# Routed rows of a two-expert layer: weighted on their way out of PSUM and added to the output in device memory tile by tile, in place of a store, a gather and a mix at the end

## What is computed

```
xn     = layernorm(x2)                       # 1024 tokens, 512 numbers each
probs  = softmax(xn @ Wg)                    # 8 experts
topv, topi = top_k(probs, 2);  topv /= sum(topv)
shared = gelu(xn @ W1) @ W2                  # every token
moe    = sum over the token's two experts e of topv_e * (gelu(xn @ Wu[e]) @ Wd[e])
out    = x2 + shared + moe
```

## Time and profile before

| | |
|---|---|
| median of 3 runs | 1807.81 us (1804.14 to 1808.26) |
| profiled execution | 1820.21 us, of which the span of the core's instructions is 1818.4 us |
| mean granted clock of TensorE | 0.957 |
| TensorE matmuls | 1668.8 us busy, 92% of the span |
| TensorE weight loads | 1310.3 us, 72% |
| VectorE, ScalarE, GpSimd | 653.6, 649.2 and 518.5 us (36%, 36%, 29%) |
| device memory | 107.27 MB read, 27.00 MB written |

### The profile page before, as it was taken

How to read it: one execution, slowest core, us unless ns; L and a number is a source line. 1 busy time by engine, 2 the same in 40 slices (tenths; PEclk the granted TensorE clock), 3 DMA queues, 4 the chain that set the end, 5 groups by cost and what they waited for, 6 DMA issues and landing times. The chain is left out here.

```text
span 1818.4 us, 24358 instructions
## 1 busy us (share of the span) xinstructions
PE 1668.8 (92%) x9230; PEld 1310.3 (72%) x9231; DVE 653.6 (36%) x1065; ACT 649.2 (36%) x1184; POOL 518.5 (29%) x291
## 2 busy tenths in 40 slices
PE   3899999999999999999999999779776989999992
PEld 2587887887887887887887887534344768888882
DVE  4224424424424524524524524331443512122123
ACT  0134434434434434434434434314222314354520
POOL 4333033033033033033033030030111254484803
PEclk9999999999999999999999999889876989999996
DMA  7511011011011011111011100260001444465315
GB/s 260 184 47 47 30 46 46 29 46 46 29 46 46 29 46 46 29 46 46 29 46 46 29 23 0 77 241 1 1 1 58 165 147 127 133 202 162 133 40 156
DMA packets 69581, 134.66 MB, mean 74 GB/s; under 512 B 7152, under 2 KB 23600, under 8 KB 69552
## 3 DMA queue, kind: packets, MB, share of 16 engines
q1 hardware_dynamic: 36048, 92.07, 15.1%
q10 hardware_dynamic: 30944, 33.83, 5.8%
q0 software_dynamic: 2560, 8.39, 1.5%
HBM read 107.27 MB, written 27.00 MB: 74 GB/s over the span
## 5 line engine op out<-in xcount | busy, mean ns | idle before, releaser
L203 POOL TENSOR_TENSOR ctx_h<-stage,one 128x1024 fp32r<-128x1024 f32 x64 | 121.3, 1895 | 769.8 <-PE ps_t L254 753.6
L254 PE MATMUL ps_s<-ctx_h,wk 128*128 128x512 f32 x1024 | 321.3, 390 | 1.7 <-DVE kT L434 1.7
L254 PE MATMUL ps_t<-wv,ctx_h 128*128 128x512 f32 x1024 | 317.4, 391 | 3.7 <-ACT vt L391 3.7
L452 DVE TENSOR_TENSOR kT<-ps_s,kT 64x512 fp32r<-64x512 f32 x128 | 87.6, 684 | 449.4 <-ACT kT L386 448.6
L254 PEld LDWEIGHTS ps_t<-wv,ctx_h 128*128 128x128 f32 x1024 | 193.4, 189 | 44.5 <-ACT vt L391 4.1
L254 PEld LDWEIGHTS ps_s<-ctx_h,wk 128*128 128x128 f32 x1024 | 192.2, 188 | 42.1 <-issue 2.5
L460 DVE TENSOR_REDUCE smax<-ps_s 128x1 f32<-128x1024 f32 x128 | 150.6, 1219 | 145.9 <-PE ps_s L267 144.9
L254 PE MATMUL ps_t<-wv,ctx_l 128*128 128x512 f32 x512 | 200.1, 391 | 0.0
L254 PE MATMUL ps_s<-ctx_l,wk 128*128 128x512 f32 x512 | 199.2, 389 | 0.0
L377 ACT ACTIVATE probs<-ps_s,nmax 128x1024 f32<-128x1024 f32 x128 | 142.1, 1124 | 91.5 <-DVE nmax L463 91.5
L385 ACT ACTIVATE kT<-ps_s 64x512 fp32r<-64x512 f32 x128 | 76.0, 594 | 265.2 <-PE ps_s L254 248.8
(11 more groups left out here) (191 smaller groups left out, 2249.0 us busy)
## 6 DMA issues: line engine op xcount, KB each, us to landing
stage<-in_ctx_dram SPq DMA_DIRECT2D x64, 512.0 KB, 3.6
raw_u<-in_up_dram SPq DMA_DIRECT2D x36, 512.0 KB, 3.4
raw_d<-in_down_dram SPq DMA_DIRECT2D x36, 512.0 KB, 4.4
row<-rows_scratch ACTq DMA_DIRECT2D x31, 256.0 KB, 2.7
rows_scratch<-zero SPq DMA_DIRECT2D x25, 256.0 KB, 3.5
rows_scratch<-y ACTq DMA_DIRECT2D x22, 256.0 KB, 3.1
q_scratch<-kT ACTq DMA_DIRECT2D x4, 1024.0 KB, 5.9
qa<-q_scratch ACTq DMA_DIRECT2D x32, 128.0 KB, 2.9
```

Source lines behind the costliest of these rows:

```text
L203: nc.gpsimd.tensor_tensor(hi, stage[:, slot], one[:, 0:1].unsqueeze(2).broadcast_to([P, 2, QT]), ALU.mult).then_inc(hi_done, 1)
L254: mm = nc.tensor.matmul(out, w(c), m(c), start=(c + k == 0), stop=(c == DC - 1 and k == 2))
L452: nc.vector.tensor_tensor(kT[XD:P, 0, p, keys], ps_s[0:XD, p, :], kT[0:XD, 0, p, keys], ALU.subtract)
```

## The change

- A table `meta_dram` has for each slot of the routed tiles the token's number and its weight. SP fills it with the number 1024 (no token) and the weight 0; GpSimd then scatters the real entries with 16 indirect transfers, and SP loads the whole table into `tag`, 31 tiles by 128 rows of two numbers.
- VectorE evicts a routed tile from PSUM with a multiplication by the rows' weights, and copies the tile's 128 token numbers to `target`. It does so only when the add of the tile before has landed (`added`) and the table is in (`tags_in`).
- GpSimd adds `y` to the output in device memory with one indirect accumulating transfer per tile (`add_rows`); rows with number 1024 are out of bounds and left out. A one-column operation on `hold` stands ahead of it.
- SP stores `x2 + shared` as the output after each shared tile. The first six of these stores stand between the weight loads of sets 1 and 2, the last two behind set 2, then the load of `tag`, then sets 3 to 8.
- GpSimd makes the rests of an expert's up chunks, adds the first tile, makes the rests of the down chunks and adds the other tiles. It starts with set 2 only when the table is loaded and the eight output stores have landed.
- The store of `y`, the gathers, the mixing and the last eight stores are gone.

```diff
@@ SP @@
-            for s in range(1, E + 1):
+            def store_out(t):
+                sp.wait_ge(y_copied, t + (AHEAD + 1))
+                sp.dma_start(out_ap[t], x2[:, t, :]).then_inc(out_stored, 16)
+
+            sp.wait_ge(tags_set, 1)
+            sp.dma_start(meta_dram.rearrange("(p r) w -> p r w", p=P), pad[:, :, :]).then_inc(padded, 16)
+            load_raw(1)
+            for t in range(NT - 2):
+                store_out(t)
+            load_raw(2)
+            for t in range(NT - 2, NT):
+                store_out(t)
+            sp.wait_ge(added, 16 * 2 * NT)
+            sp.dma_start(tag[:, 0:MAX_TILES, :], meta_dram.rearrange("(r p) w -> p r w", p=P)).then_inc(tags_in, 16)
+            for s in range(3, E + 1):
                 load_raw(s)
-            for t in range(NT):
-                sp.wait_ge(mixed, 2 * (t + 1))
-                sp.dma_start(out_ap[t], x2[:, t, :]).then_inc(out_stored, 16)
             sp.wait_ge(out_stored, 16 * NT)
@@ GpSimd @@
+            def add_rows(t):
+                pool.wait_ge(y_copied, t + (AHEAD + 1))
+                nc.gpsimd.tensor_tensor(hold[:, bass.ds(t, 1)], hold[:, 0:1], hold[:, 0:1], ALU.add)
+                pool.indirect_dma_start(
+                    out=out_ap.rearrange("b t d -> (b t) d"),
+                    out_offset=bass.IndirectOffsetOnAxis(
+                        ap=target[:, :], axis=0),
+                    in_=y[:, :], in_offset=None, bounds_check=B * T - 1, oob_is_err=False,
+                    compute_op=ALU.add).then_inc(added, 16)
...
-            for s in range(1, E + 1):
-                weights_rest(s)
-            pool.wait_ge(lo_done, CH * (E + 1))
-            pool.wait_ge(rows_sent, 16 * 2 * NT)
-            end = pool.value_load(first_i[0:1, E:E + 1], min_val=NT, max_val=MAX_TILES)
-            pool.wait_ge(row_in, end * 16 + 32)
-            pool.wait_ge(y_stored, end * 16)
-
-            nc.gpsimd.tensor_tensor(hold[:, :], hold[:, :], hold[:, :], ALU.add)
+            weights_rest(1, range(CH))
+            pool.wait_ge(tags_set, 2)
+            pool.wait_ge(padded, 16)
             for t in range(NT):
                 for k in range(2):
                     pool.indirect_dma_start(
-                        out=picked[k][:, t, :], out_offset=None,
-                        in_=rows_dram.rearrange("n p d -> (n p) d"),
-                        in_offset=bass.IndirectOffsetOnAxis(ap=slot_i[:, k, t:t + 1], axis=0)).then_inc(got[t], 16)
+                        out=meta_dram, out_offset=bass.IndirectOffsetOnAxis(ap=slot_i[:, k, t:t + 1], axis=0),
+                        in_=tags[:, k, t, :], in_offset=None).then_inc(added, 16)
+            pool.wait_ge(firsts_done, 1)
+            pool.wait_ge(tags_in, 16)
+            pool.wait_ge(out_stored, 16 * NT)
+            for e in range(E):
+                lo, hi = bounds(pool, e)
+                if e + 2 <= E:
+                    weights_rest(e + 2, range(DC))
+                add_rows(lo)
+                if e + 2 <= E:
+                    weights_rest(e + 2, range(DC, CH))
+                with pool.Fori(lo + 1, hi) as t:
+                    add_rows(t)
+            end = pool.value_load(first_i[0:1, E:E + 1], min_val=NT, max_val=MAX_TILES)
+            pool.wait_ge(row_in, end * 16 + 32)
+            pool.wait_ge(rows_sent, 16 * 2 * NT)
+            pool.wait_ge(added, end * 16 + NT * 16)
+            nc.gpsimd.tensor_tensor(hold[:, 1:2], hold[:, 0:1], hold[:, 0:1], ALU.add)
@@ ScalarE @@
-                    store(t - 1)
                     tile(t)
-            store(act.value_load(first_i[0:1, E:E + 1], min_val=NT, max_val=MAX_TILES) - 1)
@@ VectorE @@
-            nc.vector.memset(y[:, :], 0.0)
+            nc.vector.memset(pad[:, :, 1:2], 0.0)
+            nc.vector.memset(pad[:, :, 0:1].bitcast(U32), B * T).then_inc(tags_set, 1)
...
+            for k in range(2):
+                link(nc.vector.tensor_copy(tags[:, k, :, 0].bitcast(U32), token[:, :]))
+                ins = nc.vector.tensor_copy(tags[:, k, :, 1], weight[:, :, k])
+            ins.then_inc(tags_set, 1)
...
                     dve.wait_ge(down_done, t + 1)
-                    dve.wait_ge(y_stored, t * 16)
-                    nc.vector.tensor_copy(y[:, :], down_ps[:, :]).then_inc(y_copied, 1)
-
-            for t in range(NT):
-                dve.wait_ge(got[t], 32)
-                for k in range(2):
-                    nc.vector.scalar_tensor_tensor(out=x2[:, t, :], in0=picked[k][:, t, :], scalar=weight[:, t, k:k + 1],
-                                                   in1=x2[:, t, :], op0=ALU.mult, op1=ALU.add).then_inc(mixed, 1)
-                    if k == 0:
-                        dve.wait_ge(mixed, 2 * t + 1)
+                    dve.wait_ge(added, t * 16 + NT * 16)
+                    dve.wait_ge(tags_in, 16)
+                    nc.vector.tensor_copy(target[:, :], tag[:, bass.ds(t, 1), 0:1].rearrange("p o w -> p (o w)").bitcast(U32))
+                    nc.vector.tensor_scalar(y[:, :], down_ps[:, :], tag[:, bass.ds(t, 1), 1:2].rearrange("p o w -> p (o w)"),
+                                            None, ALU.mult).then_inc(y_copied, 1)
```

More of the change, by code:

```diff
@@ L1051, in _, with experts @@
                 copy(nc.vector.tensor_copy(logits[:, s, :], bank(f"lg{s}")[:, 0:E]), f"lg{s}")
-def experts(nc, up_ap, down_ap, out_ap, rows_dram, x2, xn3, logits, raw_u, raw_d, hu0, hd0, raw_in, hi_done, one):
+def experts(nc, up_ap, down_ap, out_ap, rows_dram, meta_dram, x2, xn3, logits, raw_u, raw_d, hu0, hd0, raw_in, hi_done, one):
     with ExitStack() as ctx:
@@ L1084, in experts @@
         y = sb("y", [P, D])
-        picked = [xn3, raw_u[:, :, :].rearrange("p c (h d) -> p (c h) d", d=D)]
-        hold = sb("hold3", [P, 1])
+        token = sb("token", [P, NT])
+        tags = sb("tags", [P, 2, NT, 2])
+        pad = sb("pad", [P, MAX_TILES, 2])
+        hold = sb("hold3", [P, MAX_TILES + 1])
+        target = sb("target", [P, 1], U32)
+        tag = sb("tag", [P, MAX_TILES + 1, 2])
         iota = sb("iota", [P, E])
@@ L1134, in experts @@
         y_copied = sem("y_copied")
-        y_stored = sem("y_stored")
-        got = [sem(f"got{t}") for t in range(NT)]
-        mixed = sem("mixed")
+        tags_set = sem("tags_set")
+        padded = sem("padded")
+        tags_in = sem("tags_in")
+        added = sem("added")
         out_stored = sem("out_stored")
@@ L1165, in _ @@
         def _(pool):
-            pool.sem_inc(y_stored, 16 * (NT - 1))
             pool.memset(ident[:, :], 0.0).then_inc(consts, 1)
@@ L1170, in _ @@
             pool.memset(hold[:, :], 0.0).then_inc(consts, 1)
+            pool.iota(token[:, :], pattern=[[P, NT]], base=0, channel_multiplier=1,
+                      allow_small_or_imprecise_dtypes=True).then_inc(consts, 1)
             pool.iota(iota[:, :], pattern=[[1, E]], base=0, channel_multiplier=0,
@@ L1175, in _ @@
                       allow_small_or_imprecise_dtypes=True).then_inc(consts, 1)
-            pool.wait_ge(consts, 6)
+            pool.wait_ge(consts, 7)
             pool.affine_select(out=ident[:, :], in_=ident[:, :], compare_op=ALU.not_equal, fill=1.0, base=0,
@@ L1180, in _, with weights_rest @@
                                pattern=[[-1, P]], channel_multiplier=1).then_inc(consts, 1)
-            def weights_rest(s):
-                for i in range(CH):
+            def weights_rest(s, chunks):
+                for i in chunks:
                     pool.wait_ge(hi_done, s * CH + (i + 1))
@@ L1272, in tile @@
                 mm.then_inc(down_done, 1)
-            pe.wait_ge(consts, 8)
+            pe.wait_ge(consts, 9)
             turn(0)
@@ L1298, in round_row @@
                 nc.scalar.activation(rowT_h[:, :, :], rowT_ps[:, :, :], ACT.Copy).then_inc(rowTh_done, 1)
-            def store(t):
-                act.wait_ge(y_copied, t + (AHEAD + 1))
-                act.dma_start(rows_dram[bass.ds(t, 1)].rearrange("o p d -> (o p) d"), y[:, :]).then_inc(y_stored, 16)
             def round_weights(s, first):
@@ L1405, in _ @@
             link(nc.vector.tensor_copy(index_f[:, :, :], index[:, :, 0:2]))
-            dve.wait_ge(consts, 8)
+            dve.wait_ge(consts, 9)
             for k in range(2):
@@ L1466, in perceiver_block @@
     o_dram = nc.dram_tensor("o_scratch", (B, P, PAIRS, T), F32, kind="Internal").ap()
+    meta_dram = nc.dram_tensor("meta_scratch", (MAX_TILES * P, 2), F32, kind="Internal").ap()
     rows_dram = nc.dram_tensor("rows_scratch", (MAX_TILES + 2, P, D), F32, kind="Internal").ap()
@@ L1483, in perceiver_block @@
                        x2, xn3, logits, raw_u, raw_d, hu, hd, raw_in, hi_done, one)
-        experts(nc, up, down, out, rows_dram, x2, xn3, logits, raw_u, raw_d, hu, hd, raw_in, hi_done, one)
+        experts(nc, up, down, out, rows_dram, meta_dram, x2, xn3, logits, raw_u, raw_d, hu, hd, raw_in, hi_done, one)
 def kernel(**inputs):
```

## The result

| | before | changed |
|---|---|---|
| median | 1808.03 us (4 runs, 1804.14 to 1808.29) | 1785.54 us (4 runs, 1783.23 to 1788.40) |
| ratio | | 0.9884, 95% interval 0.9870 to 0.9899 |
| profiled execution, span | 1820.2 us, 1818.4 us | 1783.2 us, 1781.3 us |

The changed kernel is 22.5 us faster; the forecast was 1784.2 us, in a range of 1780 to 1798. A later pairing on another chip gave only 9 us, by one of the rivals (experiment 6).

The account below looks back on a forecast made before the run. TensorE was taken to bound the routed stage, with a 33.45 us serial tail behind it. Gain 25.9 less 2.3 less 0 is 23.6; 1820.2 became 1796.6, less 12.4 between profile and median 1784.2 us, range 1780 to 1798.

Parts of the forecast that it names:

- Tail: After the last product: 33.45 us removed, one tile's way out of 7.5 us in its place, gain 25.9.
- Late gelus: Routed stage, two-tile experts: the down half behind the first add makes a gelu 0.8 us late, three times; cost 2.3.
- 1.75 for the add, 9.46 for the down half: GpSimd in a two-tile expert: the first add holds it 1.75 us, the down half's rests 9.46, done at 1622.1.
- Tag load: SP's load of 3968 pieces of 8 B after the last shared store, from about 1523.8; cost 0 (0 to 2.0).
- X: Length of the load of the tag table, taken near 10 us; up to 13.4 costs nothing.
- Cadence of adds: Routed tiles: VectorE's next y waits for the add before to land; 5.27 us, up to 16.3 free; cost 0.
- stores: Eight output stores move to SP in the shared tiles; set 2's loads, 11.5 us, in by about 1512; cost nothing.
- tags on VectorE: Two small fills replace one; four small copies, some 0.2 us each, fall where VectorE waits for TensorE; cost nothing.
- A: GpSimd falls behind: building an accumulating transfer holds it 3.0 us in place of 1.0; 1795 us; chance 0.12.
- C: The tag load is late: at 18 us the first adds are 4.6 us over the slack; 1789 us; chance 0.08.
- D: Routed tiles: adds slow in themselves, 17.3 us a tile gives 1816 us, 18 us gives 1831; chance 0.13.
- B: Shared tiles: tag scatters starve the other engines, as beside the row scatters (11.8 us over cadence); 1796 us; chance 0.10.

Follow-up runs that it names:

- experiment 6: The changed kernel, rests_first, and rests_first without the addition, on a third chip: 1809.55, 1804.89 and 1803.76 us, against 1818.64 for the kernel before.
- no_mixing: The kernel before without its gathers, its mixing and the waits for them, output stored before the end: 1779.54 us, ratio 0.9849.
- changed: The changed kernel run again without an edit, as the mark for the runs beside it: 1787.37 us, ratio 0.9880.
- second_set_late: The changed kernel with the eight weight loads of set 2 behind all eight output stores, in place of behind six: 1801.33 us, ratio 0.9976.
- rests_first: The changed kernel with GpSimd making the rests of two of the four down chunks before adding an expert's first tile: 1783.69 us, ratio 0.9870.
- before_again: The kernel before, without an edit, profiled a second time: 1808.03 us.
- experiment 7: rests_first with its tag scatters spread out, two behind each of the eight rests of expert 1, on a fourth chip: 1784.36 us, ratio 0.9875.
- no_adding: The changed kernel with its 21 transfers writing the weighted rows over the output rows instead of adding: 1780.78 us, ratio 0.9854.
- rests_later: The changed kernel with one more GpSimd operation of 128x1024 between the first add and the down half of each expert: 1797.65 us, ratio 0.9940.

## Why the prediction was right, and where it was off

- **Tail**: forecast 7.5, measured 8.2. The landing, as GpSimd sees it, took 4.7 in place of 5.27; VectorE started 0.28 after the product, not 0.11; and 1.3 us lie between the last hold and the span's end, a term that my sum left out. Shown by the traces, and by no_mixing in the medians of runs.
- **Late gelus**: the mechanism, its three places and its partners (ScalarE waiting for `raw_d`, TensorE at the transposes) came as forecast; the size was 3.6 to 4.0 us of waits (1.0 to 1.5 each, where I had 0.8) and 4.2 to 4.8 of the stage in place of 2.3; the 0.6 to 0.8 between waits and stage stays unexplained. The step that was mis-sized is "1.75 for the add, 9.46 for the down half". GpSimd's timeline in the changed kernel has, for that expert:

```profile
1595.05 0.19 POOL L1209 TENSOR_TENSOR hold<-hold 128x1 f32 x1 [0.64 <-DVE y L1491]
1596.09 1.57 POOL L1210 DMA_INDIRECT out_dram<-y,target  x1 [0.85 <-issue]
1597.13 10.01 POOL L1203 TENSOR_TENSOR ld<-raw_d,hd 128x1024 fp32r<-128x1024 f32 x4
```

  From hold to the end of the block that is 12.1 us where I had 11.2: 0.3 more ahead of the transfer, and 0.55 in the block, which starts while the 1.57 us of the transfer still run. The gelu also starts 0.3 to 0.5 us after ScalarE's last rounding ends, where my sum had nothing. The reload was a little quicker than my 4.4 (3.3 to 4.0 in the chain of changed), which took some of it back.
- **Tag load**: X was put at 10 and measured 4.7 us (4.2 in changed; 11.3 in second_set_late, where eight weight loads stand just ahead of it). It cost nothing, as forecast, with more room than I gave it. The pace of 623 packets in 2 us was no bound: 3968 pieces of 8 B went faster.
- **Cadence of adds, stores, tags on VectorE**: nothing, as forecast. For the first rests_first shows slack in use; for the second the changed kernel's waits show no late up load, and second_set_late that this hangs on their place. The cover is thinner than the prediction's 11.5 us for the eight loads of set 2 makes it. The issues of their down chunks in changed, and the landing of the last ones:

```profile
L1159 SPq DMA_DIRECT2D raw_d<-in_down_dram x4: 693/902/1438, 1486.2 to 1489.2; - x4
...
DMA to landing us min/median/max: 19.5/19.7/20.0
```

  The first of the eight is issued at 1484.3 and the last lands at 1509.2, so they take 24.9 us, with the tag scatters running beside the first half; ScalarE rounds the last of them from 1511.4 on, 2.2 us later. For the third the shared tiles take 88.9 to 89.1 us, 88.9 in before_again.
- **Rivals**: A (3.0 us to build an add) happened for about a quarter of its 2.0 us, 1.57 in place of 1.00, and that is part of what the late gelus were over. C and D are false: X was 4.7 against 13.4, and the landing 4.8 against 16.3. **B happened**, on one of the chips. Its argument against, that tags carry 8 B a row where rows carry 2 KB, fell: the holes are 11.5 to 11.9 us in the row scatters and 9.3 to 12.3 in the tag scatters. That the scatters cause them is not shown (experiment 7). The 1796 worked out for it is for one hole where the kernel before has none; on that chip the kernel before has, by its time, one hole as well, and what B takes is the ratio: 0.9952 in place of 0.9884.
- **Sum**: 25.9 less 2.3 was 23.6; the traces give 25.2 less 4.2 to 4.8, so 20.4 to 21.0, and the runs 22.5 and 20.3. The terms were off by 0.7 and by about 2, in the same direction, so the sum was 2.6 to 3.2 too high. That the result lies only 1.3 us from 1784.2 is luck in part: the runs of that pair gained 1.5 to 2.1 us more than the traces account for, those of the next pair did not. The 12.4 us between the profiled execution and the median, which I took over as a lump, was mostly the hole of 11.8, which before_again doesn't have.

## What to carry to other kernels

Where a serial tail of small transfers follows the last product, moving each piece of it beside the tile that produces it takes the whole tail but one piece, provided the in-order engine that issues the transfers has nothing late queued behind them: ask what stands behind each new wait, and put the work with the earliest due time ahead of it. A gain measured on one chip need not be that of the next: pair the kernels on several, and when two profiles differ by more than the runs, cut both at the same events before explaining the difference.

## What the hardware showed that I had not expected

- An accumulating indirect transfer of 128 rows of 2 KB costs GpSimd 1.57 us to build where a plain one costs 1.00, and lands in 4.8 us where that one lands in 2.7 (medians of changed and no_adding).
- 16 scatters of 128 pieces of 8 B each land after 7.4 us in the median (8.1 in changed), where those of rows of 2 KB take 2.9. It isn't the size alone: in changed those issued before 1480 us land after 3.2 in the median, and those from 1483 on, with the weight loads of set 2 under way, after 8.9. Issuing them costs the same 0.96 us.
- Waits of 3.3 to 3.9 us on TensorE (rests_later) were each followed by a stretch at 1.2 GHz, which together cost some 4 to 5 us more; waits of up to 1.5 us (changed) by none.
- On one chip of those used, three engines stop inside each row of sixteen scatters, and the tile takes 9 to 12 us longer (7.2 us of standing still and a stretch at 1.2 GHz in the hole looked at); the same profiles lack records of landings. The cause is open.
